# Stacking the high and low parts of queries and keys: DMAs through a DRAM scratch tensor instead of 0/1 matmuls

## The chip, the cores and the metric

The kernel runs as one program on one core of a Trainium2 chip. The metric is the device time of one execution in microseconds (us). Before the change it is 1311.22 us, the median of three runs.

## The reference

The input x has 16 batches of 256 tokens with 256 features; a context of the same shape supplies keys and values. What is computed, cut to what matters:

```python
x = x + tanh(g_xattn) * attention(layernorm(x), ctx, ctx)      # 16 heads of 16, biases on q, k, v, o
x = x + tanh(g_ffn) * experts(layernorm(x))                    # 8 experts, the best 2 of each token

scores = einsum('bhqd,bhkd->bhqk', qh, kh) / sqrt(16)          # attention
out = einsum('bhqk,bhkd->bhqd', softmax(scores), vh)

g = x @ gate_w.T ; u = x @ up_w.T                              # one expert, inner size 1024
y = (silu(g) * u) @ down_w.T                                   # weighted by softmax of the two best bids
```

Everything is fp32. The kernel gets near fp32 accuracy for the scores from the faster fp32r matmul by splitting each operand into a high part (rounded to fp32r) and the rest, and adding three products: high by high, rest by high, high by rest.

## The kernel before

**Two stages.** The attention stage goes over the 16 batches and ends with the rows scattered by expert into a DRAM tensor (`dispatched`); the expert stage works through tiles of 256 tokens. The change touches the attention stage alone.

**The stacks.** A head has 16 dimensions (`DK`), and two heads at a time (a "pair", 8 pairs a batch) go through the score matmuls. Each head of a pair owns 64 partitions (`STACK`): 16 rows for each of the three terms, then one row (row 48, `SHIFT`) that holds minus the maximum of the scores on the query side and 1 on the key side, so that one matmul contracts over all three terms and subtracts the maximum. `q[par]` and `k[par]` hold these stacks for all 8 pairs of one batch, in two copies by the parity `par` of the batch. The projection, however, gives the dense layout (`dense`, `high`, `rest`: 128 partitions, 2 halves `c` of 4 pairs each), so rows have to move between partitions. Before, `stack(b, what, c, n)` on TensorE (L466 to L475) does this with 8 matmuls by 0/1 matrices (`picks`) into the PSUM tile `scores`, and `read_stack` on ScalarE (L678 to L683) copies the 1024 columns out to `q` or `k`. There are four such stacks a batch: K0, K1, Q0, Q1. Since `scores` is one buffer, they take turns with the eight score units S0 to S7 (`UNITS`), guarded by the semaphores `unit_written` and `unit_read`.

**The loop.** Every engine runs `body(b, ...)` for b = 0 to 15 (`over_batches`); 0, 1, 14 and 15 are written out, 2 to 13 are a loop of two batches a turn. Body b scores batch b, finds the maxima of batch b + 1 (`max_scores`, L477), and projects, splits and stacks batch b + 2 (only if `ahead`, that is in bodies 0 to 13). TensorE's order in body b is written out by hand (L600 to L647):

- values of b + 1; maxima 0; heads turned; scores 0; maxima 1; **keys of b + 2 projected** (`project_k`, waits for `ctx_loaded`); scores 1; maxima 2; x turned; scores 2; weigh 0; scores 3; maxima 3; attention output; scores 4; maxima 4; ranks; **stack K0**; weigh 1; scores 5; **queries of b + 2 projected**; maxima 5; scores 6; weigh 2; maxima 6; scores 7; maxima 7; **stack K1**; weigh 3; the maxima turned (`turn_maxima`); **stack Q0**; router logits; **stack Q1**.

ScalarE follows with the exponentials (`exps`, L667), the copies out of PSUM and the dense queries and keys (`read_q`, `read_k`). GpSimd makes `high` and `rest` (`split`, L1058). VectorE takes the maxima and, at the end of body b, copies the turned maxima of b + 1 to `max_rows` (L880).

**SyncE's queue.** SyncE issues the DMAs in program order; a wait holds up all that is behind it. In body b it issues (L405 to L413): `load_ctx(b + 2)`, once the last misc unit of body b - 1 is written; `store_residual(b - 1)`; `store_shift(b + 1)`, two DMAs of 8 KB that put `max_rows` into row 48 of the query stacks, which `score(b + 1, 0)` waits for (`shifted`). The context that `load_ctx` loads at the start of body b is the one that `project_k(b + 2)` reads in that same body.

**The prologue** makes the stacks of batches 0 and 1 on TensorE and the maxima of batch 0; SyncE loads the weights, constants, `pick_rows` (1 MB, the 0/1 matrices) and all of x (14 DMAs of 256 KB after the first two) and then issues `store_shift(0)`.

## Time and profile before

| | |
|---|---|
| runs | 1310.25, 1311.22, 1314.03 us; median 1311.22 |
| span of the profiled execution | 1313.1 us |
| instructions | 25666 |
| TensorE matmul, busy | 1158.8 us (88%) |
| VectorE, ScalarE, GpSimd, busy | 672.9, 552.5, 361.3 us |
| mean granted TensorE clock | 0.937 of full |
| DMA | 50753 packets, 73.46 MB |

The profiled execution has no time beside its span of 1313.1 us; that span is 1.9 us (0.14%) above the median of the runs and within their scatter. Busy time of TensorE counts a matmul from its start to its modelled end, so a busy TensorE is not one at its peak; the page splits the span into 40 slices of 32.8 us, about one batch of the attention stage each, which takes slices 1 to 17.

### The profile page before, as it was taken

Reading aid. Unit: us, or ns where it says so; the run is one execution under the profiler, and the core shown is the slowest. Engines: PE = TensorE matmul, PEld = TensorE weight load, DVE = VectorE, ACT = ScalarE, POOL = GpSimd, SP = SyncE. Lnnn points to the kernel's source line nnn. Section 1 sums busy time; section 2 is a strip of 40 time slices with the busy share of each in tenths; the row PEclk is TensorE's granted clock in tenths of the full one; section 3 lists DMA queues with packets and bytes.
Section 4 is the critical chain, followed back from the end, with each engine's and each line's share of the span. In section 5 each row is a group of like instructions: output and inputs, shape, how many; then the busy total and the mean of one; then the engine's idle time right before and its main releaser. Section 6 shows DMA issues by size and latency. Waiting matters only on the chain.

```text
span 1313.1 us, 25666 instructions
## 1 busy us (share of the span) xinstructions
PE 1158.8 (88%) x9261; PEld 1021.7 (78%) x9261; DVE 672.9 (51%) x1536; ACT 552.5 (42%) x863; POOL 361.3 (28%) x385
## 2 busy tenths in 40 slices
PE   5789888888888888618897999999997999999995
PEld 4556666666666665418897999999997999999995
DVE  2546666666666665445756444444456444444442
ACT  3456565566555554424544232323334323232331
POOL 2112333344334331223534211111133111111111
PEclk7789998999899997758998999999998999999998
DMA  9000111011011100135535321211223222111121
GB/s 319 15 10 26 35 34 33 33 33 38 33 34 42 38 33 27 42 117 200 155 93 157 87 33 29 33 29 24 33 34 114 34 33 33 29 32 30 24 33 24
DMA packets 50753, 73.46 MB, mean 56 GB/s; under 512 B 6288, under 2 KB 42384, under 8 KB 50576
## 3 DMA queue, kind: packets, MB, share of 16 engines
q0 software_dynamic: 20544, 44.05, 14.2%
q1 hardware_dynamic: 29072, 27.65, 7.0%
q10 hardware_dynamic: 1088, 1.11, 0.3%
q8 instruction: 30, 0.49, 0.2%
q14 instruction: 19, 0.16, 0.0%
HBM read 47.11 MB, written 25.43 MB: 55 GB/s over the span
## 4 chain that ended last, share of the span: by engine, by line
PE 44%; DVE 5%; issue 3%; ACT 2%; DMA 1%; POOL 0%; DVEq 0%; POOLq 0%; ACTq 0%
PE gate L1213 15%; PE up L1213 15%; PE down L1229 14%; DVE w_lo L104 4%; ACT h_hi L1273 1%; PE turned L1202 1%; DVE h L1299 1%; ACT w_hi L99 1%; DMA stage<-up_T 1%; DMA out<-y,token 0%; DVE x_lo L1291 0%; DVE h_lo L1301 0%; POOL out L1348 0%; POOL stage L86 0%; DVE y L1314 0%
## 5 line engine op out<-in xcount | busy, mean ns | idle before, releaser
L1348 POOL DMA_INDIRECT out<-y,token x76 | 119.6, 1573 | 495.8 <-DVE y L1314 364.8
L1268 ACT ACTIVATE silu<-gate 128x512 f32<-128x512 f32 x152 | 90.6, 596 | 334.3 <-PE up L1213 334.3
L1299 DVE TENSOR_TENSOR h<-silu,up 128x512 f32<-128x512 f32 x152 | 104.2, 686 | 220.0 <-ACT silu L1268 220.0
L1229 PE MATMUL down<-w_hi,h_hi 128*128 128x256 f32 x608 | 176.4, 290 | 18.4 <-DVE h_lo L1301 18.2
L873 DVE TENSOR_REDUCE max_neg<-maxps 128x4 f32<-128x1024 f32 x128 | 156.4, 1222 | 60.7 <-PE maxps L487 59.1
L1301 DVE TENSOR_TENSOR h_lo<-h,h_hi 128x512 fp32r<-128x512 f32 x152 | 117.9, 776 | 109.6 <-ACT h_hi L1273 109.6
L1229 PE MATMUL down<-w_hi,h_lo 128*128 128x256 f32 x608 | 171.8, 283 | 0.0
L1229 PE MATMUL down<-w_lo,h_hi 128*128 128x256 f32 x608 | 171.5, 282 | 0.0
L675 ACT ACTIVATE probs<-scores 128x1024 f32<-128x1024 f32 x128 | 132.0, 1032 | 90.4 <-PE scores L506 90.3
L1273 ACT ACTIVATE h_hi<-h 128x512 fp32r<-128x512 f32 x152 | 96.0, 631 | 128.7 <-DVE h L1299 128.1
L1213 PE MATMUL gate<-x_hi,w_hi 128*128 128x256 f32 x608 | 125.0, 288 | 12.4 <-issue 7.9
L1229 PEld LDWEIGHTS down<-w_hi,h_hi 128*128 128x128 f32 x608 | 115.2, 189 | 22.1 <-DVE h_lo L1301 21.6
L1213 PE MATMUL gate<-x_lo,w_hi 128*128 128x256 f32 x608 | 124.0, 286 | 0.0
L1213 PE MATMUL up<-x_hi,w_hi 128*128 128x256 f32 x608 | 123.3, 284 | 0.0
L1213 PE MATMUL up<-x_hi,w_lo 128*128 128x256 f32 x608 | 123.1, 284 | 0.0
L1213 PE MATMUL gate<-x_hi,w_lo 128*128 128x256 f32 x608 | 123.1, 284 | 0.0
L1213 PE MATMUL up<-x_lo,w_hi 128*128 128x256 f32 x608 | 122.6, 283 | 0.0
L1229 PEld LDWEIGHTS down<-w_lo,h_hi 128*128 128x128 f32 x608 | 115.3, 190 | 0.0
L1229 PEld LDWEIGHTS down<-w_hi,h_lo 128*128 128x128 f32 x608 | 115.3, 190 | 0.0
L1213 PEld LDWEIGHTS gate<-x_hi,w_hi 128*128 128x128 f32 x608 | 95.6, 193 | 14.3 <-issue 14.1
L1213 PEld LDWEIGHTS gate<-x_lo,w_hi 128*128 128x128 f32 x608 | 95.7, 193 | 0.0
L1213 PEld LDWEIGHTS gate<-x_hi,w_lo 128*128 128x128 f32 x608 | 95.4, 192 | 0.0
(153 smaller groups left out, 2162.6 us busy)
## 6 DMA issues: line engine op xcount, KB each, us to landing
xg<-dispatched SPq DMA_DIRECT2D x39, 272.0 KB, 2.8
stage<-gate_T POOLq DMA_DIRECT2D x8, 1024.0 KB, 5.5
stage<-up_T POOLq DMA_DIRECT2D x8, 1024.0 KB, 7.1
stage<-down_T POOLq DMA_DIRECT2D x8, 1024.0 KB, 6.3
x_all<-x SPq DMA_DIRECT2D x16, 256.0 KB, 4.6
ctxT<-ctxT SPq DMA_DIRECT2D x16, 256.0 KB, 2.7
out<-x_all SPq DMA_DIRECT2D x16, 256.0 KB, 2.1
out<-y,token POOLq DMA_INDIRECT x76, 3.8
```

The costliest lines, as they stand in the source:

```text
L99: nc.scalar.activation(hi[:, part(n, half)], stage[:, part(n, half)], ACT.Copy).then_inc(s_hi, 1)
L104: eng.tensor_tensor(lo[:, part(n, half)], stage[:, part(n, half)], hi[:, part(n, half)].bitcast(fp32), ALU.subtract).then_inc(s_split[n], 1)
L675: nc.scalar.activation(probs[g % 2][:, at:at + HPP].rearrange("p u t s -> p (u t) s"), scores[:], ACT.Exp).then_inc(s["unit_read"], 1)
L873: V.tensor_reduce(to, maxps[:], AX.X, ALU.max, negate=True).then_inc(s["max_taken"], 1)
L1202: last = nc.tensor.transpose(turned[:, c, t * P:(t + 1) * P], xg[:, t, c * P:(c + 1) * P], idn[:])
L1213: last = mm(bank[:, i, :], weights(par, w, mat)[:, c, cols], r[:, c, :], start=m == 0, stop=m == len(terms) - 1)
L1229: last = mm(down[t][:, 0:D], r[:, i, t * P:(t + 1) * P], weights(par, w, 2)[:, i, :], start=i == 0 and m == 0, stop=i == IC - 1 and m == 2)
L1268: nc.scalar.activation(silu[pair % 2][:], gate[pair % 2][:], ACT.Silu).then_inc(s_silu, 1)
L1273: nc.scalar.activation(h_hi[:, 2 * pair:2 * pair + 2, :], h[pair % 2][:], ACT.Copy).then_inc(s_hhi, 1)
L1299: V.tensor_tensor(h[pair % 2][:], silu[pair % 2][:], up[pair % 2][:], ALU.mult).then_inc(s_made, 1)
L1301: V.tensor_tensor(h_lo[:, 2 * pair:2 * pair + 2, :], h[pair % 2][:], h_hi[:, 2 * pair:2 * pair + 2, :].bitcast(fp32), ALU.subtract).then_i ...
L1348: pool.indirect_dma_start(out, bass.IndirectOffsetOnAxis(token[:, t:t + 1], axis=0), y[:, t, :], None, compute_op=ALU.add).then_inc(s_adde ...
```

## The change

The 0/1 matmuls, the copies out of PSUM, the tile `picks`, `ones_row`, `pick_rows` and the four stack units go. In their place SyncE writes the dense `high` and `rest` to a DRAM tensor `parts`, 2 DMAs of 256 KB for queries and 2 for keys, and reads them back into the stacks: `stack(par, what, c, ...)` issues 6 DMAs (3 terms by 2 heads), each of 16 partitions by 4 pairs by 256 columns, 64 KB. A batch has 4 stores and 24 loads. The tiles `q` and `k` are filled once by VectorE (0 and 1), which gives the row of ones. TensorE waits on `stacked0` before maxima 0 of a batch and on `stacked1` before maxima 4. ScalarE and GpSimd wait on the stores (`Q_parts_stored`, `K_parts_stored`) before they overwrite `high`. `project_q` and `read_q` move ahead of scores 5 and `exps(b, 5)`. The prologue's maxima of batch 0 are no longer mixed with projections and stacks. The core of the diff:

```diff
+    parts = nc.dram_tensor("parts", [2, 2, 2, HC, P, SEQ], fp32, kind="Internal").ap()
...
-            load(((probs[0][:], pick_rows),), "picks_loaded")
...
-            for b in range(2, BATCHES):
-                load_x(b, "x_rest_loaded")
+            def store_parts(b, par, what, splits, landed):
+
+                sp.wait_ge(s["q_split" if what == "Q" else "k_split"], splits)
+                if not is_first(b):
+                    sp.wait_ge(s[f"{what}_parts_stored"], landed)
+                for n, part in enumerate((high, rest)):
+                    sp.dma_start(parts[par, "QK".index(what), n].rearrange("c p s -> p c s"),
+                                 part[what][:].bitcast(fp32)).then_inc(s[f"{what}_parts_stored"], 16)
+
+            def stack(par, what, c, landed):
+
+                if c == 0:
+                    sp.wait_ge(s[f"{what}_parts_stored"], landed)
+                to = (q if what == "Q" else k)[par]
+                for n, part in enumerate(TERMS[what]):
+                    for u in range(HPP):
+                        row_ = u * STACK + n * DK
+                        of = parts[par, "QK".index(what), part, c, u * STACK:(u + 1) * STACK]
+                        sp.dma_start(to[row_:row_ + DK, c * BLOCKS:(c + 1) * BLOCKS, :].bitcast(fp32),
+                                     of.rearrange("(i d) s -> d i s", d=DK)).then_inc(s[f"stacked{c}"], 16)
+
+            for b in range(2):
+                for what in "KQ":
+                    store_parts(b, b, what, b + 1, b * PARTS_LAND)
+                    if b == 0 and what == "K":
+                        sp.wait_ge(s["stacks_empty"], 1)
+                    for c in range(HC):
+                        stack(b, what, c, (b + 1) * PARTS_LAND)
+                if b == 0:
+                    for later in range(2, BATCHES):
+                        load_x(later, "x_rest_loaded")
             store_shift(0, 0, PRO1)
...
             def body(b, par, use, ahead, nxt, back, late):
 
                 if ahead:
-                    sp.wait_ge(s["misc_written"], use.before)
-                    load_ctx(b + 2, par)
+                    started, splits, contexts = kept("started", use.before), kept("splits", b + 3), kept("contexts", b * 16 + 32)
+                    before, landed = kept("before", b * PARTS_LAND + 2 * PARTS_LAND), kept("landed", b * PARTS_LAND + 3 * PARTS_LAND)
+                    half, whole = kept("half", unit(b, 3) + 1), kept("whole", unit(b, 7) + 1)
+                    sp.wait_ge(s["misc_written"], started)
+                    load_ctx(b + 2, par, contexts)
+                    store_parts(b + 2, par, "K", splits, before)
                 if back:
                     store_residual(b - 1, use)
+                if ahead:
+                    sp.wait_ge(s["unit_written"], half)
+                    stack(par, "K", 0, landed)
+                    store_parts(b + 2, par, "Q", splits, before)
+                    stack(par, "Q", 0, landed)
                 if nxt:
                     store_shift(b + 1, 1 - par, use)
+                if ahead:
+                    sp.wait_ge(s["unit_written"], whole)
+                    stack(par, "K", 1, landed)
+                    stack(par, "Q", 1, landed)
...
-            def max_scores(b, par, pair, units):
+            def max_scores(b, par, pair):
...
-                if pair == 0:
-                    pe.wait_ge(s["unit_read"], units)
+                if pair % BLOCKS == 0:
+                    pe.wait_ge(s[f"stacked{pair // BLOCKS}"], b * STACKS_LAND + STACKS_LAND)
...
-                stack_ahead("K0")
                 weigh(b, par, 1)
-                score(b, par, 5)
                 if ahead:
                     project_q(use)
+                score(b, par, 5)
                 max_of_next(5)
...
-                stack_ahead("K1")
                 weigh(b, par, 3)
                 if nxt:
                     turn_maxima(b + 1, use)
-                stack_ahead("Q0")
                 if back:
                     logits(use)
-                stack_ahead("Q1")
...
+            for i in range(2):
+                V.memset(q[i][:].bitcast(fp32), 0.0)
+                last = V.memset(k[i][:].bitcast(fp32), 1.0)
+            last.then_inc(s["stacks_empty"], 1)
```

`kept(name, value)` puts a value that depends on the loop's register into a register of its own before the waits.

## Rows read from the trace of the kernel before

**Rows 1.** The page: DMA bandwidth in each of the 40 slices

```profile
GB/s 319 15 10 26 35 34 33 33 33 38 33 34 42 38 33 27 42 117 200 155 93 157 87 33 29 33 29 24 33 34 114 34 33 33 29 32 30 24 33 24
```

**Rows 2.** Windows, four successive batches: length, engines' busy time, granted clock, DMA

```profile
271.60:302.40 30.80, 27.03 (x228) 19.63 (x228) 20.43 (x58) 18.87 (x31) 11.78 (x17) 1.00 0.11 36
302.40:332.50 30.10, 26.84 (x227) 19.45 (x227) 20.60 (x58) 18.13 (x28) 11.78 (x17) 0.99 0.10 36
332.50:366.10 33.60, 29.75 (x228) 21.61 (x228) 20.42 (x58) 18.77 (x31) 11.78 (x17) 0.91 0.10 33
366.10:397.90 31.80, 28.50 (x227) 20.90 (x227) 20.70 (x58) 18.26 (x29) 11.77 (x17) 0.95 0.10 34
```

**Rows 3.** Timeline across a batch's end: start, duration, engine, line, idle time before

```profile
261.59 0.84 ACT L711 ACTIVATE Q_dense<-misc,bqs 128x256 f32<-128x256 f32 x2 [0.90 <-PE misc L443]
...
263.50 1.28 POOL L1066 TENSOR_TENSOR Q_rest<-Q_dense,Q_high 128x512 fp32r<-128x512 f32 x1 [0.15 <-POOL Q_high L1064]
...
266.72 1.07 PE L517 MATMUL pv<-probs,values 128*32 128x256 f32 x16
...
269.84 1.35 SPq L391 DMA_DIRECT2D queries<-max_rows  x2
...
270.89 0.17 DVE L884 TENSOR_TENSOR z<-misc,cb_s 128x16 f32<-128x16 f32 x1 [1.08 <-PE misc L551]
...
271.57 0.40 SPq L362 DMA_DIRECT2D ctxT<-ctxT  x1
...
271.87 0.39 PE L473 MATMUL scores<-Q_high,picks_Q high 128*128 128x256 f32 x1 [1.87 <-ACT queries L682]
...
272.92 1.89 PE L458 MATMUL misc<-wv_s,ctxT 128*128 128x256 f32 x8
```

**Rows 4.** TensorE's timeline of the next batch

```profile
277.22 1.99 PE L443 MATMUL misc<-ctxT,wk_s 128*128 128x256 f32 x8
...
288.35 1.07 PE L517 MATMUL pv<-probs,values 128*32 128x256 f32 x16
289.62 0.50 PE L506 MATMUL scores<-queries,keys 64*128 64x256 f32 x4 [0.20 <-ACT keys L682]
290.05 1.99 PE L443 MATMUL misc<-xT,wq_s 128*128 128x256 f32 x8
...
297.21 1.07 PE L517 MATMUL pv<-probs,values 128*32 128x256 f32 x16
```

**Rows 5.** Groups by line, two turns of the loop (206.2 to 458.8)

```profile
L675 ACT ACTIVATE probs<-scores 128x1024 f32<-128x1024 f32 x64 | 66.2, 1034 | 42.9 <-PE scores L506 42.9
```

**Rows 6.** SyncE's instructions for the context tile: ns min/median/max, first and last start

```profile
L362 SPq DMA_DIRECT2D ctxT<-ctxT x16: 378/398/434, 1.7 to 458.8; - x16
L362 SPq MOVE ctxT<-ctxT x12: 29/36/39, 113.5 to 458.7; - x12
```

**Rows 7.** DMA issues of the page: KB each, median us from issue to landing

```profile
ctxT<-ctxT SPq DMA_DIRECT2D x16, 256.0 KB, 2.7
out<-x_all SPq DMA_DIRECT2D x16, 256.0 KB, 2.1
```

**Rows 8.** SyncE's timeline of the prologue

```profile
19.13 0.43 SPq L356 DMA_DIRECT2D tok<-token_no  x1
19.60 0.43 SPq L356 DMA_DIRECT2D pads<-pad_rows  x1
20.08 8.50 SPq L352 DMA_DIRECT2D x_all<-x  x14
52.77 1.53 SPq L391 DMA_DIRECT2D queries<-max_rows  x2
```

**Rows 9.** Timeline of the last batch's start: scores that wait for the shift

```profile
520.02 1.32 SPq L391 DMA_DIRECT2D queries<-max_rows  x2
...
522.66 0.80 PE L506 MATMUL scores<-queries,keys 64*128 64x256 f32 x4 [1.14 <-DMA queries<-max_rows]
```

**Rows 10.** Window at the start of one batch: engines' busy time, clock, DMA

```profile
332.00:334.00 2.00, 1.21 (x5) 1.21 (x6) 1.10 (x4) 0.84 (x2) 0.20 (x2) 0.50 0.24 49
```

More of the change, by code:

```diff
@@ L173, in attention_stage @@
         k = [sb(f"keys{i}", [P, HPAIRS, SEQ], f32r) for i in range(2)]
-        picks = {what: sb(f"picks_{what}", [P, BLOCKS, P], f32r) for what in ("Q high", "Q rest", "K high", "K rest")}
-        ones_row = sb("ones_row", [P, 1])
         max_neg = sb("max_neg", [P, QT, HEADS])
@@ L263, in read, with unit @@
                 eng.wait_ge(misc_read[n], uses + 1)
-        UNITS = ["S0", "S1", "S2", "S3", "S4", "K0", "S5", "S6", "S7", "K1", "Q0", "Q1"]
-        STACKS = ["K0", "K1", "Q0", "Q1"]
-        def units_before(b):
-            last = isinstance(b, int) and b == BATCHES - 1
-            return b * len(UNITS) + (2 * len(STACKS) if not last else len(STACKS))
-        def unit(b, what):
-            order = [n for n in UNITS if n not in STACKS] if isinstance(b, int) and b >= BATCHES - 2 else UNITS
-            return units_before(b) + order.index(what)
-        def first_stack_unit(b, what):
-            return b * len(STACKS) + STACKS.index(what)
+        def unit(b, pair):
+            return b * HPAIRS + pair
+        TERMS = {"Q": (0, 1, 0), "K": (0, 0, 1)}
+        PARTS_LAND, STACKS_LAND = 2 * 16, 2 * 3 * HPP * 16
         def after_all(use):
@@ L350, in _, with kept @@
         def _(sp):
+            registers = {}
+            def kept(name, value):
+                if isinstance(value, int):
+                    return value
+                if name not in registers:
+                    registers[name] = sp.alloc_register("sp_" + name)
+                sp.reg_mov(registers[name], value)
+                return registers[name]
             def load_x(b, loaded="x_loaded"):
@@ L464, in write_unit @@
                     pe.wait_ge(s["unit_read"], n)
-            def stack(b, what, c, n):
-                if c == 0:
-                    pe.wait_ge(s["q_split" if what == "Q" else "k_split"], b + 1)
-                write_unit(n)
-                for i in range(BLOCKS):
-                    mm(scores[:, i, :], picks[what + " high"][:, i, :], high[what][:, c, :], start=True, stop=False)
-                    last = mm(scores[:, i, :], picks[what + " rest"][:, i, :], rest[what][:, c, :], start=False, stop=True)
-                last.then_inc(s["unit_written"], 1)
-            def max_scores(b, par, pair, units):
-                if pair == 0:
-                    pe.wait_ge(s["unit_read"], units)
+            def max_scores(b, par, pair):
+                if pair % BLOCKS == 0:
+                    pe.wait_ge(s[f"stacked{pair // BLOCKS}"], b * STACKS_LAND + STACKS_LAND)
                 if not (is_first(b) and pair == 0):
@@ L568, in _ @@
             project_q(PRO0)
-            pe.wait_ge(s["picks_ready"], 1)
-            def stack_first(b, what):
-                stack(b, what[0], int(what[1]), first_stack_unit(b, what))
-            for what in STACKS:
-                stack_first(0, what)
             pe.wait_ge(s["consts_loaded"], 16 * NCONST)
@@ L580, in _ @@
             turn_x(1, PRO1)
-            max_scores(0, 0, 0, len(STACKS))
             project_k(1, 1, PRO1)
-            max_scores(0, 0, 1, len(STACKS))
             project_q(PRO1)
-            for pair in range(2, HPAIRS):
-                max_scores(0, 0, pair, len(STACKS))
-                if pair < 6:
-                    stack_first(1, STACKS[pair - 2])
+            for pair in range(HPAIRS):
+                max_scores(0, 0, pair)
             turn_maxima(0, PRO1)
@@ L593, in max_of_next @@
                     if nxt:
-                        max_scores(b + 1, 1 - par, pair, units_before(b))
-                def stack_ahead(what):
-                    if ahead:
-                        stack(b + 2, what[0], int(what[1]), unit(b, what))
+                        max_scores(b + 1, 1 - par, pair)
                 if nxt:
@@ L752, in _ @@
                 high_part(b, "Q", use)
-                for what in STACKS:
-                    read_stack(b, what[0], int(what[1]), first_stack_unit(b, what))
                 if b == 0:
@@ L948, in _ @@
             stats_x(0)
-            dve.wait_ge(s["picks_loaded"], 16)
-            loaded = probs[0][:].rearrange("p m t (h c) -> p m (t h) c", c=P)
-            for n, what in enumerate("QK"):
-                for m, part in enumerate(("high", "rest")):
-                    last = V.tensor_copy(picks[f"{what} {part}"][:], loaded[:, 2 * n + m])
-            last.then_inc(s["picks_ready"], 1)
+            for i in range(2):
+                V.memset(q[i][:].bitcast(fp32), 0.0)
+                last = V.memset(k[i][:].bitcast(fp32), 1.0)
+            last.then_inc(s["stacks_empty"], 1)
             stats_x(1)
```

66 lines of the change are left out of this document (21 added, 45 removed).

## The prediction

> **What bounds the kernel now.** I read the windows of single batches first, then the timeline across a batch's end, then SyncE's own instructions. The attention stage is the only part that changes; the expert stage is left at what it is. A batch takes 30.1 to 33.6 us, and TensorE is busy for 27 to 30 us of it, ScalarE for 18 to 19, VectorE for 20 to 21, GpSimd for 12 [rows 2]. So TensorE's order sets the batch, with short waits. The largest lies at the batch's end: 1.87 us before stack Q1, because `scores` is one buffer and ScalarE must first copy Q0 out [rows 3]. The same four windows show the price of such gaps: at a granted clock of 1.00 or 0.99 a batch takes 30.8 and 30.1 us, at 0.91 it takes 33.6, at 0.95 31.8 [rows 2]. In the 33.6 us batch the clock stands at 0.50, the lower of its two levels (1.2 GHz), right after TensorE's pause at the batch's end [rows 10]. Four batches take 126.3 us against 120.4 at 30.1 each: 1.5 us a batch go to slow restarts.
>
> SyncE's queue today has slack: the two shift DMAs start at 269.84, the next context at 271.57, 1.35 us before the values matmuls that open the next batch (272.92) and 5.65 us before the key projection that reads it (277.22) [rows 3, 4]. A context lands 2.7 us after its issue [rows 7]; the cover is 3 us.
>
> **What the change saves on TensorE.** I take the values matmuls as time 0 of a batch (272.92, the next would be 303.36, so 30.44 us) and redo TensorE's order. Weigh 1 stands at 15.43, scores 5 at 16.70, the query projection at 17.13, weigh 3 at 24.29 [rows 4].
> - A stack costs TensorE 1.05 us (271.87 to 272.92) [rows 3]. Without K0, weigh 1 starts at 14.4. The query projection now follows it directly: 14.4 + 1.27 = 15.65, and takes 1.99: 17.6. ScalarE reads it for 0.84 us [rows 3] to 18.5, and only then comes exponential 5, 1.03 us [rows 5], to 19.5. Before, that exponential ran ahead of the read. Scores 6 waits for it, exponential 6 ends at 20.6 or a little later, the two normalisations and the copy of weigh 2 (1.5 us together) come ahead of exponential 7, which ends at 23.6. Weigh 3 starts at 23.7, against 24.29. Two stacks are gone (2.1 us), but 0.6 us is gained: the new order gives the rest back.
> - From weigh 3 to the next values: 6.20 us before. VectorE reads the logits at 270.89, 4.17 us after weigh 3 [rows 3]; less Q0 (1.05) that is 3.1, plus some 0.1 for the values to follow: 3.2. The wait and Q1 are gone.
> - The batch is then 23.7 + 3.2 = 26.9 us, 3.5 less than 30.44. It happens in 14 bodies: 49 us. Bounds: 2.5 us (the chains below take up their small margins) and 4.5 us (the new order costs nothing).
>
> ScalarE loses four copies of about 1.05 us a batch; as it has 12 us idle, that is worth nothing beyond the above.
>
> **The trip of Q0 through DRAM.** `read_q` starts at 17.7; GpSimd has `rest` of the queries 3.2 us after the read starts (261.59 to 264.78) [rows 3]: 20.9. SyncE issues two stores, 0.47 us apart (19.13 to 19.60 in the prologue) [rows 8]; the second lands at 20.9 + 0.5 + 2.1 = 23.5 [rows 7]. Six loads at 0.47 take SyncE to 26.3, the last lands at 28.5 if it takes 2.7 from its issue like a context. Maxima 0 of the next body is due 1.82 after its values, at 28.7. So this is just hidden. The shift follows the same rows as now: 3.12 us after weigh 3 [rows 3], at 26.8, when SyncE is free; scores 0 can start 2.64 us after it [rows 9], at 29.4, and is due at 29.7. Hidden too, both by 0.2 to 0.3 us; that thin cover is why the lower bound of the saving is 2.5.
>
> **What the change moves: the context load.** After the shift, SyncE issues K1 and Q1, 12 DMAs, and only then comes body b + 1 with its `load_ctx`. All 12 have their waits met (scores 7 is long written), so their cost is issue time. The trace has no 64 KB load of this shape; the nearest is the context's issue, 0.38 to 0.43 us [rows 6], and 0.47 from one to the next in a row [rows 8]. I take 0.47, so 5.64 us. Bounds are 0.38 us, the fastest context issue, and 0.67, from the shift pair's 1.35 us for two [rows 3]. The shift starts about 0.1 before the next values and lasts 1.35, so: +1.27, then 5.64 to 6.9, then the seven values that are put into registers (some ten moves of 0.036 us [rows 6], an estimate) to 7.2. Landing 2.7 later: 9.9. The key projection is due at 4.30 and would start at 10.0. It holds scores 1 and everything behind it on TensorE, hence the exponentials, the maxima, and the next shift: nothing hides it. **A new stall of 5.7 us in bodies 1 to 13: 74 us.** (Body 0 has no stacks right ahead of its context; bodies 14 and 15 load none.) At the bounds it is 4.6 and 8.1 us: 60 and 105.
>
> The chains above start behind this stall and move with it, so their margins hold.
>
> **The clock.** A gap of 1.9 us is followed by a slow restart in some batches and costs 1.6 us (31.8 against 30.1) to 3.5 us (33.6). With 5.7 us idle in every batch I take 2.5 us, the middle, in all 13, against 1.5 in the mean now: 13 us more. Bounds 0 and 26. The Trainium skill, "TensorE: Matmul & The Clock Gate", section "HAM oscillation — how this bites in real kernels", tells of a kernel that waits for a DMA in each round and comes back at the low clock every single time; by it the term is this 13, by the rows' present share of slow restarts it would be 0 and the sum 1349.
>
> **The prologue.** Without `pick_rows` (1 MB at the 319 GB/s of the first slice [rows 1]: about 3 us) SyncE could reach the end of the constants (20.03 now [rows 8]) at 17. Then, all in line on SyncE: K stores of batch 0, issued and landed, 3.5 us (to 20.5); 12 loads, 5.6 (26.1); Q stores 3.1 (29.2); 12 loads (34.8). TensorE has eight maxima to do from there, as before. SyncE goes on: 14 loads of x, 8.5 us [rows 8] (43.3); K stores of batch 1, landed behind 3.7 MB of x at about 320 GB/s (11.5 us from 34.8, plus 2): 48.5; 12 loads (54.1); Q stores (57.2); 12 loads (62.8); then the shift, which was issued at 52.77 [rows 8]. That is 10 us later; with TensorE restarting at the low clock 11. Bounds 6 and 16. The fill by VectorE (4 tiles) lies ahead of anything that waits for it.
>
> **The sum**, against the profiled execution's own span: 1313.1 + 11 + 74 + 13 - 49 = 1362 us. The median of the runs stands 2 us below that span, so I predict 1360 us. 0.3% (4 us) is about what a measurement of this kernel can tell from no change.
>
> **The rivals.**
> - *A, the forecast*, 0.70: the late context stalls the key projection. 1345 to 1380 by itself.
> - *B, the small DMAs are dearer*, 0.13: 0.67 us each. The stall is 8.1 (105 us); Q0's six take 4.0, so SyncE is free at 27.5, the shift is 0.7 late, 0.4 beyond its margin (6 us); the prologue's 48 cost 0.2 each more (10). 1313 + 21 + 105 + 13 + 6 - 49 = 1409. For it: DMAs that touch few partitions, the shift's, are the slow ones [rows 3]. Against: they touch one partition, these 16.
> - *C, cheap issues*, 0.10: a quarter of a context's rows at 0.33 each. The stall is 4.0 (52), prologue 4, clock 5: 1325. Against: today's issues of 1 KB and of 256 KB take equally long, so size hardly matters.
> - *D, faster*, 0.05: issuing costs next to nothing, the 12 loads take 1.2 us, the stall 1.2 (16), prologue 2, clock 0: 1313 + 2 + 16 - 49 = 1282. It decides below about 0.2 us a DMA, where 13 stalls and the prologue equal the 49 saved. Nothing in rows 6 or 8 is near it. The Trainium skill, "DMA: Bandwidth & Descriptors", section "Issuing engines are not separate DMA queues", calls the time to initiate a DMA usually small relative to the DMA itself; taken at its word for 12 in a row this is D, and the trace disagrees: 0.47 against 2.7 is a sixth, and twelve of them are twice a landing.
> - *E, in between*, 0.02: the change moves little because gain and stall cancel, 1311.
>
> The range 1325 to 1400 leaves out D, E and most of B, with the edge of C. Chances: faster by over 0.3% 0.05, within 0.03, slower 0.92.
>
> **What the profile after would show.** Right: in bodies 1 to 13 the key projection idles about 5.7 us until the DMA of the context; the context's issue lies some 7 us after the values matmuls instead of 1.35 before; SyncE issues one small load each 0.47 us; the wait at the batch's end is gone; the clock is below 0.95 in most batches; the first shift is issued at 63; batches last 34 to 35 us. Wrong: a longer wait at maxima 0 for Q0 (the trip through DRAM is dearer than two landings), batches near 27 us (D), or exponential 5 not late.

## The result and the profile after

The kernel takes **1376.3 us** after the change (median of four runs, 1374.9 to 1378.6); four runs of the kernel before on that chip give 1312.6 us (1310.3 to 1314.0). The ratio is 1.050, 95% interval 1.0479 to 1.0521: slower by 64 us.
First the page after: clock and DMA in 40 slices, the group of the key projection, and the landings (beside [rows 1] and [rows 7]).

```profile
PEclk8578877988868888775799999999999999999998
...
GB/s 224 201 89 97 104 103 99 107 103 104 94 93 104 106 97 102 93 41 105 170 155 120 133 103 31 32 31 31 31 31 120 22 32 31 31 31 31 31 31 23
...
L485 PE MATMUL misc<-ctxT,wk_s 128*128 128x256 f32 x128 | 56.8, 621 | 66.0 <-DMA ctxT<-ctxT 66.0
...
keys<-parts SPq DMA_DIRECT2D x192, 64.0 KB, 2.2
...
ctxT<-ctxT SPq DMA_DIRECT2D x16, 256.0 KB, 2.7
```

The DMA rate of a batch has tripled to some 100 GB/s and is still far from the 319 of [rows 1]: bandwidth isn't what is short. A small load lands in 2.2 us and a context in 2.7, as before [rows 7]. The line of the key projection carries 66 us of idle time that it didn't have. SyncE's timeline shows where they come from (from the first shift shown to the next, stores of the residual and one more pair of stores left out; [rows 3] has the same place before):

```profile
201.48 1.35 SPq L391 DMA_DIRECT2D queries<-max_rows  x2
202.87 2.78 SPq L411 DMA_DIRECT2D keys<-parts  x6
205.69 2.77 SPq L411 DMA_DIRECT2D queries<-parts  x6
209.75 0.40 SPq L363 DMA_DIRECT2D ctxT<-ctxT  x1
221.23 0.38 SPq L399 DMA_DIRECT2D parts<-K_high  x1
...
233.86 2.70 SPq L411 DMA_DIRECT2D queries<-parts  x6
238.12 1.37 SPq L391 DMA_DIRECT2D queries<-max_rows  x2
```

Twelve loads take SyncE from 202.87 to 208.46, 0.47 us from one to the next, and they wait for nothing: this is issue time. Another 1.3 us later the context is issued, then it sits idle for 11 us. The values matmuls of this batch stand at 201.61, so the context goes out 8.1 us behind them (7.1 to 9.5 in the other batches), where it went out 1.35 us ahead of them before [rows 3]. TensorE's timeline of the same batch:

```profile
201.61 3.34 PE L500 MATMUL misc<-wv_s,ctxT 128*128 128x256 f32 x8
...
212.53 3.77 PE L485 MATMUL misc<-ctxT,wk_s 128*128 128x256 f32 x8 [5.09 <-DMA ctxT<-ctxT]
...
229.53 0.50 PE L536 MATMUL scores<-queries,keys 64*128 64x256 f32 x4 [1.18 <-ACT probs L686]
...
232.12 0.80 PE L517 MATMUL maxps<-keys,queries 48*128 48x256 f32 x4 [1.09 <-DVE max_neg L867]
...
238.87 2.48 PE L500 MATMUL misc<-wv_s,ctxT 128*128 128x256 f32 x5
```

The key projection waits 5.09 us and then takes 3.77 us; before, the same eight matmuls took 1.99 [rows 4]. Two shorter waits follow. Windows inside this batch (columns as in [rows 2]) give the clock around each: full at first while TensorE idles, half after the long wait, full again by 229, and half from the wait at 231 on through the batch's end.

```profile
208.00:210.00 2.00, 0.00 (x0) 0.00 (x0) 1.29 (x3) 0.35 (x1) 0.00 (x0) 1.00 0.36 104
...
213.00:215.00 2.00, 2.00 (x6) 1.55 (x6) 0.00 (x0) 0.00 (x0) 0.00 (x0) 0.50 0.00 0
...
229.00:231.00 2.00, 1.47 (x20) 0.71 (x20) 1.90 (x6) 1.40 (x3) 1.74 (x2) 1.00 0.13 37
...
234.00:236.00 2.00, 2.00 (x18) 1.00 (x20) 1.03 (x2) 1.01 (x2) 1.39 (x3) 0.50 0.54 163
```

**Where the 64 us went.** The two shift DMAs of a batch cut the span alike in both traces: the first shift is issued at 52.77 before [rows 8] and at 68.78 after; the shift at the end of body 12 at 457.04 and 527.78; the last at 520.02 [rows 9] and 593.73. So the prologue grew by 16.0 us, bodies 0 to 12 by 54.7 (404.27 to 459.00), bodies 13 and 14 by 3.0, and the rest, the last body and the expert stage, shrank by 10.0. Together 63.7. For bodies 0 to 12 the window over the whole stretch splits busy from idle, before and then after:

```profile
52.77:457.04 404.27, 358.76 (x2900) 258.62 (x2899) 252.42 (x666) 236.24 (x367) 142.50 (x208) 0.95 0.10 32
```

```profile
68.78:527.78 459.00, 341.92 (x2478) 233.81 (x2479) 262.83 (x660) 185.47 (x315) 142.85 (x205) 0.83 0.32 102
```

TensorE is idle for 45.5 us before and 117.1 after: +71.6. It is busy for 16.8 us less, though 52 stacks of 1.05 us [rows 3], 54.6 us, are gone: the other 37.8 us are the same matmuls running slower, at a clock of 0.83 instead of 0.95. That makes -54.6 + 37.8 + 71.6 = +54.8. The split is good to some 2 us: 51 of the 52 stacks start inside the stretch, and a few ran slower than 1.05 us. Counted matmul by matmul, the time in which TensorE worked on stacks alone is 56.5 us here (39.6 of slowing) and 52.6 in the trace of `before_here` below, by which the slowing of the other rows without stacks is 2.0 lower. The waits of TensorE in that stretch (line, releaser, total us, times, longest), before and then after, say which idle time changed:

```profile
PE scores L473 <- ACT queries L682: 19.9, 12, 1.9
PE scores L506 <- ACT probs L675: 8.1, 14, 0.9
...
PE maxps L487 <- DVE max_neg L873: 2.4, 2, 1.3
```

```profile
PE misc L485 <- DMA ctxT<-ctxT: 62.3, 13, 6.8
PE scores L536 <- ACT probs L686: 20.8, 24, 1.2
PE maxps L517 <- DVE max_neg L867: 14.3, 14, 1.5
PE scores L536 <- DMA queries<-max_rows: 5.9, 4, 3.0
...
PE maxps L517 <- DMA queries<-parts: 3.8, 3, 2.2
```

### The profile page after: what moved, and what is told of

Its sections match the earlier page's. It is cut to its first block, busy times and chain, and to the rows that moved or that the text cites. A ratio compares the mean times of both kernels' runs of the same rounds, so it can differ in the third digit from the quotient of the medians.

```text
span 1376.8 us, 24968 instructions
## 1 busy us (share of the span) xinstructions
PE 1129.1 (82%) x8749; PEld 981.8 (71%) x8749; DVE 692.9 (50%) x1536; ACT 488.9 (36%) x799; POOL 360.2 (26%) x385
## 3 DMA queue, kind: packets, MB, share of 16 engines
q1 hardware_dynamic: 76912, 68.57, 16.3%
## 4 chain that ended last, share of the span: by engine, by line
PE 41%; DVE 5%; issue 3%; ACT 2%; DMA 1%; POOL 0%; DVEq 0%; POOLq 0%; ACTq 0%
PE gate L1205 14%; PE up L1205 14%; PE down L1221 13%; DVE w_lo L105 3%; ACT h_hi L1265 1%; PE turned L1194 1%; DVE h L1291 1%; DMA stage<-up_T 1%; ACT w_hi L100 1%; DMA out<-y,token 0%; DVE x_lo L1283 0%; DVE h_lo L1293 0%; POOL out L1340 0%; POOL stage L87 0%; DVE y L1306 0%
## 5 line engine op out<-in xcount | busy, mean ns | idle before, releaser
L1293 DVE TENSOR_TENSOR h_lo<-h,h_hi 128x512 fp32r<-128x512 f32 x152 | 125.8, 828 | 110.7 <-ACT h_hi L1265 110.7
L485 PE MATMUL misc<-ctxT,wk_s 128*128 128x256 f32 x128 | 56.8, 621 | 66.0 <-DMA ctxT<-ctxT 66.0
L517 PE MATMUL maxps<-keys,queries 48*128 48x256 f32 x512 | 67.2, 345 | 51.8 <-DVE max_neg L867 28.2
L517 PEld LDWEIGHTS maxps<-keys,queries 48*128 48x128 f32 x512 | 46.0, 220 | 75.6 <-DVE max_neg L867 38.0
```

The lines of the kernel that those rows point to most:

```text
L485: last = mm(use.bank(what)[:, o, :], weights[:, c, o * P:(o + 1) * P], source[:, c, :], start=c == 0, stop=c == HC - 1)
L517: last = mm(maxps[:, u, t, :], q[par][r, pair, t * P:(t + 1) * P], k[par][r, pair, :], start=True, stop=True)
L1293: V.tensor_tensor(h_lo[:, 2 * pair:2 * pair + 2, :], h[pair % 2][:], h_hi[:, 2 * pair:2 * pair + 2, :].bitcast(fp32), ALU.subtract).then_i ...
```

## The experiments

They ran on two chips. The record doesn't number the chip of the pair above; that it is a third one is read from its time alone. The kernel before takes 1281.5 us beside `ctx_first`, `six_ahead`, `before_plus_12` and `warm_wait`, 1279.5 beside `after_again`, `warm_wait_40`, `ctx_first_old_order` and `ctx_first_x_on_pool` (the same chip), and 1279.5 beside the other four (the second chip). Its batches are shorter there, 28.9 us instead of 31.1. Each ratio is against the runs of before beside it; the traces are set against that of `before_here`, which is from the second chip. The last columns split bodies 0 to 12 as above: by how much the stretch is longer than before, what of it is slower matmuls (the change in busy time, with the stacks' 54.6 us added back where they are gone), and what is more idle time; the clock is that stretch's. All splits come from one execution each, that of ctx_first from the slowest of its ten runs.

| kernel | median us | ratio (95%) | clock | bodies 0 to 12 | slower matmuls | idle |
|---|---|---|---|---|---|---|
| after, first chip | 1376.3 | 1.050 (1.048 to 1.052) | 0.83 | +54.7 | +37.8 | +71.6 |
| after_again | 1362.2 | 1.066 (1.063 to 1.069) | 0.82 | +73.1 | +52.7 | +74.9 |
| ctx_first | 1282.2 | 1.001 (0.998 to 1.004) | 0.87 | +4.0 | +34.8 | +23.8 |
| six_ahead | 1326.5 | 1.036 (1.031 to 1.041) | 0.83 | +39.3 | +54.3 | +39.6 |
| before_plus_12 | 1345.6 | 1.051 (1.048 to 1.055) | 0.92 | +62.3 | +24.7 | +37.7 |
| warm_wait | 1406.6 | 1.090 (1.083 to 1.097) | | | | |
| warm_wait_40 | 1355.9 | 1.061 (1.058 to 1.063) | 0.88 | +68.7 | +38.4 (and +56.2 added) | +28.8 |
| ctx_first_old_order | 1284.3 | 1.004 (1.002 to 1.007) | 0.92 | -1.0 | +20.1 | +33.5 |
| ctx_first_x_on_pool | 1284.2 | 1.004 (1.002 to 1.007) | 0.89 | -3.0 | +27.3 | +24.3 |
| x_late_on_pool | 1285.0 | 1.004 (1.001 to 1.007) | 0.90 | +2.0 | +26.7 | +29.9 |
| q0_half_on_act | 1279.3 | 0.995 (0.991 to 0.999) | 0.93 | -9.5 | +16.3 | +28.7 |
| q0_act_old_order | 1267.5 | 0.990 (0.987 to 0.994) | 0.92 | -16.8 | +16.5 | +21.4 |

### before_here: the kernel before, looked at on the second chip

> The kernel before, unaltered, for a trace on the chip of the other runs: its attention stage is to be set beside theirs batch by batch. Expected: 1280 us, batches of 30 to 31 us, first shift at 53 us.

One run, 1276.8 us. The window of bodies 0 to 12, the row that the splits in the table start from:

```profile
52.74:429.00 376.26, 345.97 (x2889) 249.19 (x2889) 252.37 (x666) 235.45 (x367) 141.72 (x207) 0.99 0.10 34
```

Its clock is 0.99 where the first chip's was 0.95, and its wait before stack Q1 is 4.6 us in 12, where it was 19.9. Of the 28 us between the two traces of one kernel in this stretch, 15.2 are idle time, which is that one wait (15.3). So most of the wait that the change takes away on the first chip hardly exists on this one.

### after_again: the kernel after, unaltered

> The changed kernel unaltered, beside the others on one chip, since chips differ. Both theories: the ratio to the kernel before stays 1.05, so about 1345 us where the kernel before takes 1281.

1362.2 us, 82.7 above before on this chip, against 63.7 on the first. The stretch takes 449.33 us with TensorE busy for 344.11, and the context is waited for as on the first chip:

```profile
PE misc L485 <- DMA ctxT<-ctxT: 55.4, 13, 6.4
```

The expected time of 1345 was too low, as it took the first chip's ratio. The loss is at the same place on both chips; its size isn't the same.

### ctx_first: the context ahead of the twelve loads

```diff
                     load_ctx(b + 2, par, contexts)
+                if back and nxt:
+                    sp.wait_ge(s["unit_written"], kept("whole", unit(b, 0)))
+                    stack(1 - par, "K", 1, 0)
+                    stack(1 - par, "Q", 1, 0)
+                if ahead:
                     store_parts(b + 2, par, "K", splits, before)
...
                 if nxt:
                     store_shift(b + 1, 1 - par, use)
-                if ahead:
-                    sp.wait_ge(s["unit_written"], whole)
-                    stack(par, "K", 1, landed)
-                    stack(par, "Q", 1, landed)
```

> The changed kernel with one thing moved on SyncE: the 12 loads of K1 and Q1 of a batch are issued in the next body, right behind load_ctx instead of ahead of it. Same DMAs, same bytes, same waits elsewhere. Theory 1 (the late context is the loss): the key projection starts about 4.3 us after the values matmuls again, its 5.1 us idle before it is gone, the low clock that follows is gone, and 13 batches give back 5 to 8 us each: 1376 - 65 to 1376 - 105, that is 1270 to 1310 us. Theory 2 (the trip of K and Q parts through DRAM and the added traffic are the loss, the context only waits in their company): TensorE waits as long at the maxima for the stacks instead, and the time stays above 1350.

The same DMAs, the same bytes and the same work, in another order on one queue: 1282.2 us (ten runs), 80 of the 82.7 us are gone. That is the first theory; with the second the time would have stayed above 1350. SyncE, then TensorE, in one batch:

```profile
219.36 0.41 SPq L363 DMA_DIRECT2D ctxT<-ctxT  x1
219.87 2.76 SPq L411 DMA_DIRECT2D keys<-parts  x6
222.67 2.77 SPq L411 DMA_DIRECT2D queries<-parts  x6
```

```profile
217.98 3.76 PE L501 MATMUL misc<-wv_s,ctxT 128*128 128x256 f32 x8
...
224.15 1.99 PE L486 MATMUL misc<-ctxT,wk_s 128*128 128x256 f32 x8
...
239.03 0.50 PE L537 MATMUL scores<-queries,keys 64*128 64x256 f32 x4 [1.17 <-ACT probs L687]
...
241.60 0.50 PE L518 MATMUL maxps<-keys,queries 48*128 48x256 f32 x4 [1.06 <-DVE max_neg L868]
...
243.43 0.50 PE L518 MATMUL maxps<-keys,queries 48*128 48x256 f32 x4 [0.50 <-DVE max_neg L868]
243.85 1.07 PE L548 MATMUL pv<-probs,values 128*32 128x256 f32 x16
...
246.33 1.97 PE L501 MATMUL misc<-wv_s,ctxT 128*128 128x256 f32 x8
249.34 0.51 PE L518 MATMUL maxps<-keys,queries 48*128 48x256 f32 x4 [1.03 <-DMA queries<-parts]
```

The key projection starts at 224.15 with no wait and takes 1.99 us. But the kernel is level with before, not 49 us faster. The table says why: the 54.6 us of stacks are gone, 34.8 came back as slower matmuls and 23.8 as idle time. (This trace is of the slowest of the ten runs, 7.8 us above their median, so some of that is its own: ctx_first_x_on_pool, with the same loop and a trace below its median, shows 27.3 and 24.3.) The values matmuls at 217.98 show the first: 3.76 us, against 1.97 in the next batch; the four waits of 1.17, 1.06, 0.50 and 1.03 us show the second.

### six_ahead: six loads ahead of the context, six behind

```diff
                     load_ctx(b + 2, par, contexts)
+                if back and nxt:
+                    stack(1 - par, "Q", 1, 0)
+                if ahead:
                     store_parts(b + 2, par, "K", splits, before)
...
                     sp.wait_ge(s["unit_written"], whole)
                     stack(par, "K", 1, landed)
-                    stack(par, "Q", 1, landed)
```

> The changed kernel with only the 6 loads of K1 ahead of the context and the 6 of Q1 behind it: half the dose. Theory 1: the context is issued 2.8 us earlier, and each of 13 batches is 2.8 us shorter or a little more where the clock stays up: about 1335 us, half way between the changed kernel and ctx_first. Theory 2: no change beyond noise, 1370 to 1380.

1326.5 us. With 0, 6 and 12 loads ahead of the context the time is 1282, 1326 and 1362: 44 us for the first six, 36 for the next. The steps are near enough even, 3.4 and 2.7 us a batch over 13, but they are made of different things. The first six add 14.8 us of waits for the context (4.1 to 18.9) and 20 of slower matmuls, or 27 against ctx_first_x_on_pool (34.8 or 27.3 to 54.3); the next six add 36.5 us of waits (18.9 to 55.4) and no slowing (54.3 to 52.7). So each load more makes the kernel slower, and that the steps look even is chance. Six loads are 2.8 us of issue time, so the context is late from the first few on; of the 3 us of cover before the change [rows 3, 4, 7] ctx_first already spends 2.7: its context goes out 1.4 us behind the values (217.98 to 219.36 above), not 1.35 ahead.

### before_plus_12: the kernel before with twelve loads that nobody reads

```diff
+        spare = sb("spare", [P, 2, 4, SEQ])
...
                 if nxt:
                     store_shift(b + 1, 1 - par, use)
+                if ahead:
+                    if not is_first(b):
+                        sp.wait_ge(s["spared"], b * 192)
+                    for n in range(12):
+                        sp.dma_start(spare[16 * (n % 8):16 * (n % 8) + 16, n // 8],
+                                     x[0, 64:128].rearrange("(i d) s -> d i s", d=DK)).then_inc(s["spared"], 16)
```

> The kernel before, with matmul stacks, plus 12 loads of 64 KB (16 partitions x 4 x 256, from an input to an unused tile) between store_shift and the next body's load_ctx, in bodies 0 to 13. Nothing reads them. If the issue time of 12 DMAs ahead of the context is enough by itself (theory 1), the context is issued about 5.6 us later, which is about 4.3 us after the values matmuls; landing 2.7 later it makes the key projection wait some 2.5 to 3 us more than its slack allows, and with slow restarts the time is 1312.6 + 13 x 3 to 5 = 1350 to 1378. If traffic or the DRAM round trip were the cause, this adds next to nothing: under 1320.

The loads (64 KB of x each into a tile without a reader) are extra work. The time is 1345.6 us, +64 against before (expected were 37 to 65, reckoned from 1312.6). SyncE and TensorE around the context:

```profile
253.67 5.53 SPq L419 DMA_DIRECT2D spare<-x  x12
...
254.90 1.89 PE L466 MATMUL misc<-wv_s,ctxT 128*128 128x256 f32 x8
...
259.85 0.40 SPq L363 DMA_DIRECT2D ctxT<-ctxT  x1
...
262.63 3.78 PE L451 MATMUL misc<-ctxT,wk_s 128*128 128x256 f32 x8 [3.36 <-DMA ctxT<-ctxT]
```

Twelve issues on this queue, with 0/1 matmuls still in place and no trip through DRAM, are enough: a wait of 3.36 us, and the key projection at half speed (3.78 against 1.99). The wait is shorter than in the kernel after because here the context goes out 5 us behind the values, not 8.

### warm_wait and warm_wait_40: TensorE kept busy while it waits

```diff
                 if ahead:
+                    if back:
+                        use.free(pe, "K")
+                        for _ in range(80):
+                            mm(use.bank("K")[:, 0, 0:P], ones[:], before[:], start=True, stop=True)
                     project_k(b + 2, par, use)
```

The 80 matmuls (40 in the second kernel) of 128 by 128 are thrown away: they fill the wait, and the key projection overwrites them.

> The changed kernel with 80 throwaway 128x128x128 fp32r matmuls into the free bank of the key projection before it waits for the context, in bodies 1 to 13: about 4.5 us of work in the place of 5.1 us of idle time. The context lands when it did. Theory of the clock (the restart at 1.2 GHz after the wait costs 2 to 3 us a batch): the matmuls behind the wait run at the upper level and the kernel is 25 to 40 us faster than the changed one, about 1345. Rival (the slow stretch is hidden behind other waits, or its price is small): 1370 to 1380.

80 were too many: they took 9.15 us in a batch looked at, some 4 more than the wait, and the kernel got slower, 1406.6 us, not the 1345 expected. This one tells nothing apart.

> The changed kernel with 40 throwaway matmuls ahead of the wait for the context instead of 80. The 80 took 9.15 us (0.113 each), 4 us more than the wait, so they held the key projection up themselves; 40 take 4.5 us and fit into the 5.1 us of idle time. Theory of the clock: the projection and what follows run at the upper level (1.94 us for the projection in the run with 80, 3.77 in the changed kernel), some 2.5 us a batch, 13 batches: about 33 us below after_again. Rival (price of the slow stretch small or hidden): within 8 us of after_again.

1355.9 us, 6.3 below after_again: not the 33 expected, but what the rival said. In 11 of the 13 batches it does what it was meant to, in two it doesn't; one of each:

```profile
206.43 4.68 PE L628 MATMUL misc<-before,ones 128*128 128x128 f32 x40
211.34 1.99 PE L485 MATMUL misc<-ctxT,wk_s 128*128 128x256 f32 x8 [0.22 <-DMA ctxT<-ctxT]
...
244.75 7.03 PE L628 MATMUL misc<-before,ones 128*128 128x128 f32 x32
251.58 3.51 PE L485 MATMUL misc<-ctxT,wk_s 128*128 128x256 f32 x8
```

At 211 the projection is warm (1.99 us). At 245 the clock was already down when the throwaway matmuls began, so 32 of them take 7.03 us, 0.22 each instead of 0.12, and the projection follows at 3.51. The split still sizes the term: with the 56.2 us taken off that 12 times 40 matmuls take at 0.117 each (body 0 has none), 38.4 us of slowing are left, against 52.7 in after_again, 14 less. Some 8 of the 38.4 are the throwaway matmuls' own (40 take 8.8 us instead of 4.7 in the two batches), so on the kernel's own matmuls filling the wait takes away 22. Taking the wait itself away gives 52.7 - 34.8 = 18 in ctx_first and 25 in ctx_first_x_on_pool. Why so little is gained in time: the idle time falls by 46.1 us (74.9 to 28.8), but the fill takes 56.2 itself, 10 more than it replaces, and that eats most of the 14.

### ctx_first_old_order: scores 5 ahead of the query projection again

```diff
                 weigh(b, par, 1)
+                score(b, par, 5)
                 if ahead:
                     project_q(use)
-                score(b, par, 5)
                 max_of_next(5)
...
+                exps(b, 5)
                 if ahead:
                     read_q(b + 2, use)
-                exps(b, 5)
```

> ctx_first with scores 5 and exponential 5 back ahead of the query projection and its read, as in the kernel before. Theory 3 (the new order gives the saved matmuls back): the waits of 1.17 us at scores 6 and 1.09 us at maxima 6 shrink, the clock no longer falls at the end of so many batches, and 14 batches give 1 to 2 us each: 1255 to 1268 where ctx_first takes 1282. Rival (the trip of Q0 through DRAM is the limit): the queries are ready 0.9 us later, the wait at maxima 0 (1.03 us in a fast batch of ctx_first) grows by as much, and the time is that of ctx_first or up to 12 us more.

1284.3 against 1282.2 us: no difference that these runs can tell. With everything else as in ctx_first, the order alone is worth nothing, and the rival is what came. The waits show the trade: those for the late exponentials go (6.9 us in 13, 23.6 in 28 in ctx_first), and those for the loads of Q0 come in their place (3.6 us in three in ctx_first), beside longer ones for VectorE (21.9 against 14.3).

```profile
PE maxps L518 <- DMA queries<-parts: 15.2, 9, 3.2
```

### ctx_first_x_on_pool and x_late_on_pool: the loads of x on GpSimd's queue

```diff
-                if b == 0:
-                    for later in range(2, BATCHES):
-                        load_x(later, "x_rest_loaded")
...
             scale_x(1)
+            for later in range(2, BATCHES):
+                pool.dma_start(x_all[:, later], x[later].rearrange("(t p) d -> p t d", p=P)).then_inc(s["x_rest_loaded"], 16)
```

In x_late_on_pool the same loads stand behind `add_bias(1)`, later in GpSimd's prologue.

> ctx_first with the 14 loads of x of batches 2 to 15 issued by GpSimd in the prologue instead of by SyncE between the stacks of batch 0 and those of batch 1. Theory (SyncE's line of DMAs sets the prologue): the first shift, at 68.8 us in the changed kernel, is 7.7 us of issues and some 4 us of queueing earlier, about 57 to 60, and the kernel is 8 to 12 us below ctx_first, about 1272. Rival (bytes, not issues, set the prologue): within 3 us of ctx_first.

> ctx_first with the 14 loads of x issued by GpSimd after its two bias additions (about 30 us), so that the first stores of K parts don't land behind them, as they did in ctx_first_x_on_pool (issued 17.8, the loads that wait for them at 29.1). Theory (SyncE's chain of issues and landings sets the prologue): the first shift is at 60 instead of 69 us and the kernel is 7 to 10 us below ctx_first: about 1274. Rival (the time of the prologue is given back later): within 4 us of ctx_first.

The first shift is issued at 65.26 and 69.34 (ctx_first: 69.10), and the times are 1284.2 and 1285.0 us: nothing gained, where 8 to 12 and 7 to 10 us were expected. The queue gets shorter, but the transfers collide. In ctx_first_x_on_pool SyncE issues the loads of stack K(0) 11 us after the second store, where the kernel after did it in 5.4 and ctx_first in 6.8. In x_late_on_pool K(0) takes 6.5, but the stores of Q(0) are waited for 6.3 us instead of 2.2, and then SyncE waits 7.8 us for VectorE's rest of the keys of batch 1, so its queue alone no longer sets the prologue. The first of these:

```profile
17.78 0.53 SPq L399 DMA_DIRECT2D parts<-K_rest  x1
29.07 5.51 SPq L411 DMA_DIRECT2D keys<-parts  x12
```

### q0_half_on_act and q0_act_old_order: half of Q0 issued by ScalarE

```diff
+                if ahead:
+                    act.wait_ge(s["Q_parts_stored"], b * PARTS_LAND + 3 * PARTS_LAND)
+                    for n, part in enumerate(TERMS["Q"]):
+                        act.dma_start(q[par][STACK + n * DK:STACK + n * DK + DK, 0:BLOCKS, :].bitcast(fp32),
+                                      parts[par, 0, part, 0, STACK:2 * STACK].rearrange("(i d) s -> d i s", d=DK)).then_inc(s["stacked0"], 16)
                 read_pv(b, 3)
```

Both build on x_late_on_pool; SyncE keeps the other three loads of Q0. The second also has the old order of ctx_first_old_order.

> x_late_on_pool with 3 of the 6 loads of Q0 issued by ScalarE, behind its copy of the turned x2, instead of by SyncE. Theory (in a batch without the late context, Q0's issue line is what maxima 0 waits for, 1.03 us in a fast batch): the line is 1.4 us shorter, the wait goes, 14 batches give up to 1 us each: 8 to 14 us below x_late_on_pool. Rival (ScalarE pays for it: 1.4 us of issues and a wait for the stores ahead of the copy of weigh 3): no gain, or up to 15 us slower.

> q0_half_on_act with scores 5 and exponential 5 back ahead of the query projection. Now that Q0 has 1.4 us of slack, the old order can pay: the waits of 1.17 and 1.09 us at scores 6 and maxima 6 shrink, about 1 us a batch, 10 to 14 us below q0_half_on_act. Rival: Q0 is late again and it is within 5 us of it, as ctx_first_old_order was of ctx_first.

q0_half_on_act has ten runs from 1264.0 to 1287.4 us; their median, 1279.3, is before's, so I count it as no gain shown over before. It is 5.7 us below x_late_on_pool, less than the 8 to 14 expected. q0_act_old_order gives 1263.7 to 1272.0 in four runs, and the fastest of 18 runs of before on this chip is 1274.0: faster by 1.0% (0.6 to 1.3), 11.8 below its sister as expected (10 to 14), and the only version here that beats both kernels. As its sister scatters over 23 us, the four runs are few for the size. Its queues and TensorE at a batch's end:

```profile
259.75 1.28 SPq L411 DMA_DIRECT2D queries<-parts  x3
259.76 1.32 ACTq L789 DMA_DIRECT2D queries<-parts  x3
...
261.17 1.37 SPq L391 DMA_DIRECT2D queries<-max_rows  x2
261.30 1.97 PE L498 MATMUL misc<-wv_s,ctxT 128*128 128x256 f32 x8
...
263.98 0.51 PE L515 MATMUL maxps<-keys,queries 48*128 48x256 f32 x4 [0.71 <-DMA queries<-parts]
```

Both queues issue side by side, 1.3 us instead of 2.7, and the shift goes out 0.13 us before the values. With Q0 issued in half the time the old order has more room: the waits for exponentials fall (8.4 us against 23.8), Q0 is late by 0.71 us in this batch and by 8.6 us in eight waits of the stretch (15.2 in nine in ctx_first_old_order), and the idle time of the split falls from 28.7 to 21.4 us.

## Why the prediction was right

The likeliest case was A, the late context, at 1360 us; it came, and the time is 1376.3, inside the range. That the time is only 16 us off is in part luck: the clock cost 25 us more than was taken, and 19 of that were made up by a shorter stall and by an expert stage that wasn't to change. The steps:

| term | predicted | in the two traces |
|---|---|---|
| prologue | +11 | +16.0 |
| context waited for, 13 bodies | +74 | +65.3 (5.0 a body) |
| clock | +13 | +37.8 in bodies 0 to 12 |
| TensorE's order without stacks | -49 in 14 bodies | -45.3 in bodies 0 to 12 |
| expert stage and last body | 0 | -10.0 |

**The late context is shown.** The issue cost was taken as 0.47 us and is that; the context was to go out 7.2 us behind the values and went out 8.1 behind; the stall was to be 5.7 and is 5.0 (the waits above, 62.3, less 0.7 in body 0, which doesn't count among the 13, plus 3.7 in body 13). It is shorter though the context is later, as the key projection is also due later: 5.8 us behind the values in the batch shown (212.53 less 5.09, less 201.61), not 4.3, for the values themselves run at the lower clock (3.34 us, 1.89 before). ctx_first takes away the order and with it 80 of 82.7 us; six_ahead gives the dose; before_plus_12 makes the loss without the change. B (dearer DMAs, 1409) falls with the 0.46 us an issue took, and so do C and D. The choice of 0.47 was lucky in one way: in a row the 14 loads of x had taken 8.50 us [rows 8], 0.61 each, and the prediction doesn't weigh that row for the small loads. The part that I undercut is the time between the last load and the context, 0.3 estimated: it is 0.84 us in one body of a turn of the loop and 1.2 to 1.3 in the other, where the loop jumps back (before, from the shift to the context: 0.39 and 0.73). The Trainium skill, "DMA: Bandwidth & Descriptors", section "Issuing engines are not separate DMA queues", calls the time to initiate a DMA usually small relative to the DMA itself: for one of these it is (0.46 against 2.2), for twelve in a row it isn't (5.5 us), and here they took a kernel level with before to 6.6% above it (ctx_first and after_again).

**What the stacks save was sized right on the first chip, and too high for the others.** Taken by the split: -54.6 for the stacks, and of the 71.6 us more of idle time 62.3 are the context, so 9.3 are other waits, net of the Q1 wait that went. -54.6 + 9.3 = -45.3 for 13 bodies, 3.5 each, the predicted number. Against before_here the same sum gives less: -54.6 + 74.9 - 55.4 = -35.1 in after_again, 2.7 each, and -34.9 in ctx_first, -33.9 in six_ahead, near the lower bound of 2.5. There the wait before Q1 was short already (4.6 us, 19.9 on the first chip). Of the single parts, scores 6 waits for the late exponential 5 (1.18 us) and the wait before Q1 is gone, as forecast. What I hadn't in it are the maxima 6 and 7, which wait for VectorE (1.09 and 0.50 us); in part the end of the batch makes up for them, which takes 2.5 us from weigh 3 to the next values (243.85 to 246.33 in ctx_first), not 3.2. So that the sum comes out at just 3.5 is partly chance.

**The clock was mis-sized threefold.** The step "with 5.7 us idle in every batch I take 2.5 us" (its lower end is 31.8 - 30.1 = 1.7, not 1.6) costed the context wait alone, and for that wait the 13 us are too low, but of the right order: 14 to 22 by warm_wait_40, 18 to 25 by the kernels with the context on time. The larger part is another: 27 to 35 us of slowing stay with the context on time. In the trace after, the low clock comes also at the batch's end, behind waits of 1.2 and 1.1 us, where before the stacks K1, Q0 and Q1 followed: the window at 234 shows TensorE fully busy at 0.50. The change took 54.6 us of dense work out of TensorE, put short waits there, and the remaining matmuls run slower; I had costed the removed work and not what its going does to the clock. Four kernels set the two causes side by side: with stacks and the context on time the slowing is 0, as it is counted from there (before_here), with stacks and a late context 24.7 (before_plus_12), without stacks and on time 27 to 35, without stacks and late 52.7 (after_again). That the stacks themselves kept the clock up is my reading and isn't shown: no run put other work there, and with the stacks gone in all of them the slowing still goes from 16 to 35 us by the order and the queue of Q0. The Trainium skill, "TensorE: Matmul & The Clock Gate", section "HAM oscillation — how this bites in real kernels", has each DMA wait end in a low clock; the trace agrees (the key projection's matmuls have a median of 634 ns, 379 at full clock). The price didn't go with the length of the waits here: six_ahead, whose nine context waits come to 18.9 us, is slowed as much (+54.3) as after_again with 55.4 us in 13 (+52.7), and ctx_first by 34.8 with 4.1 us.

**The prologue** took 16.0, at the upper bound of 6 to 16. The stores of K(0) went out at 18.72, not 17, and were landed 5.4 us after the second one's issue (19.20 to 24.65 in the trace after), behind constants still in flight, not 2.1; the stores of K(1) 6.5 us (47.33 to 53.86), behind x. The first shift went out at 68.78, not at 63.

**The expert stage wasn't to change and got 10 us shorter,** in both pairs of traces (from the last shift to the end 793.1 to 783.1, and 791.3 to 781.5 from before_here to after_again). 7.9 and 6.9 us of it are three pauses of the gate matmuls that are there before and not after, and for which the profile names nothing that was waited for. Why they go stays open.

The trace lies 15 us above the sum of 1362: +5 prologue, -9 context, +25 clock, +4 saving (nearly all of it body 13's 3.5, which my split leaves out), -10 expert stage.

## What to carry to other kernels

Count the DMAs that a change puts ahead of others in a queue, each at its issue time, and look up what stands behind them: it isn't bytes that are late, it is the next issue. A load that feeds the next stage goes ahead of loads that have half a batch of time, and a row of small loads can be shared out over two engines' queues (here worth something only together with the old order). Work taken off a busy TensorE isn't worth its own length when waits stand in its place: split the stretch into removed work, slower matmuls and idle time, as above, before the gain is believed.

## What the runs showed of the hardware that I hadn't expected

- The issue of a 64 KB load by 16 partitions costs SyncE 0.46 us, about what one of 16 or 136 KB (0.43 [rows 8]) or of a 256 KB context (0.38 to 0.43 [rows 6]) does. In a row the 14 loads of x were dearer, 0.61 each [rows 8].
- Two engines issue side by side: three loads on each of two queues took 1.3 us where six on one took 2.7. That helps only where the transfers don't meet others: with x on GpSimd's queue the stores of K(0) were waited for until 11 us after their issue.
- One kernel's time differs by chip (or by whatever else differed between the sessions), 1312.6 against 1279.5 us for before, and almost all of it is in the attention stage: of 38.1 us between the two traces 28.0 lie in 13 batches, 15.3 of these in one wait for ScalarE, 12.8 in busy time at a lower clock. The loss by the change differs too, 64 and 83 us.
- Runs of some versions without stacks are further apart than those of before (1274.0 to 1285.9 in 18 runs): 1264.0 to 1287.4 us for q0_half_on_act, with mean clocks of 0.944 and 0.910 in those two runs.
